# Two attentions of a transformer stack: routing split over two engines, throwaway matmuls in the prologue, and row maxima subtracted by an accumulating matmul

## The reference

```
x = x + linear_attention(layernorm(x))   # 16 heads of 8, the sums run over the sequence positions
x = x + moe(layernorm(x))
x = x + softmax_attention(layernorm(x))  # 16 heads of 8, scores / sqrt(8), softmax over 256 keys
x = x + moe(layernorm(x))
```

## Time and profile before

| | us |
|---|---|
| median of 3 runs | 580.54 (578.9 to 585.16) |
| the profiled execution | 574.57 |
| its span, first to last instruction | 572.8 |
| PE busy | 517.6 (90%) |
| DVE busy | 432.7 (76%) |
| ACT busy | 344.8 (60%) |
| POOL busy | 290.0 (51%) |
| mean granted clock of PE | 0.971 of full |

### The profile page before, as it was taken

How to read it: one execution, slowest core, us unless ns; L and a number is a source line. 1 busy time by engine, 2 the same in 40 slices (tenths; PEclk the granted TensorE clock), 3 DMA queues, 4 the chain that set the end, 5 groups by cost and what they waited for, 6 DMA issues and landing times. The chain is left out here.

```text
span 572.8 us, 11532 instructions
## 1 busy us (share of the span) xinstructions
PE 517.6 (90%) x3757; PEld 390.4 (68%) x3757; DVE 432.7 (76%) x1105; ACT 344.8 (60%) x607; POOL 290.0 (51%) x276
## 2 busy tenths in 40 slices
PE   3878887899999999999788898988999999999996
PEld 3555564577888888888454555645678888888884
DVE  3678798569798898567677887989479796886663
ACT  3676746456555655666457767676865655555553
POOL 4765572146666756777421305020166656666664
PEclk9799988899999999999779999999999999999999
DMA  6358870213454344235641524310442444354340
GB/s 168 114 185 263 245 249 2 72 62 98 107 116 127 92 119 121 98 112 180 200 117 51 185 75 143 116 39 3 62 106 97 109 135 124 103 137 132 95 143 20
DMA packets 48549, 67.60 MB, mean 118 GB/s; under 512 B 6625, under 2 KB 18930, under 8 KB 48498
## 3 DMA queue, kind: packets, MB, share of 16 engines
q1 hardware_dynamic: 45392, 66.47, 39.9%
q10 hardware_dynamic: 3106, 0.48, 0.5%
HBM read 53.56 MB, written 13.37 MB: 117 GB/s over the span
## 5 line engine op out<-in xcount | busy, mean ns | idle before, releaser
L639 POOL TENSOR_TENSOR KS<-PT,QS 128x512 fp32r<-128x512 f32 x144 | 186.2, 1294 | 118.1 <-ACT QS L836 106.1
L831 ACT ACTIVATE bank<-bank 128x512 f32<-128x512 f32 x128 | 74.5, 582 | 98.5 <-PE bank L856 97.9
L1562 DVE TENSOR_TENSOR PT<-CS,bank 128x512 f32<-128x512 f32 x128 | 87.4, 683 | 45.1 <-PE bank L856 44.3
L854 PE MATMUL bank<-XH,WH 128*128 128x512 f32 (+1 forms) x288 | 115.4, 401 | 1.7 <-DVE PT L1434 1.5
L856 PE MATMUL bank<-XH,WL 128*128 128x512 f32 (+1 forms) x288 | 112.9, 392 | 0.0
L855 PE MATMUL bank<-XL,WH 128*128 128x512 f32 (+1 forms) x288 | 112.6, 391 | 0.0
L836 ACT ACTIVATE QS<-PT 128x512 fp32r<-128x512 f32 x144 | 90.1, 626 | 12.2 <-DVE PT L1567 11.8
L1458 DVE TENSOR_REDUCE MEXP<-bank 128x4 f32<-128x1024 f32 x64 | 78.2, 1223 | 22.8 <-PE bank L966 22.1
L1567 DVE TENSOR_TENSOR PT<-PT,bank 128x512 f32<-128x512 f32 x128 | 88.0, 687 | 9.5 <-ACT bank L831 1.6
L750 ACT ACTIVATE PT<-bank 128x1024 f32<-128x1024 f32 x64 | 65.6, 1025 | 40.1 <-PE bank L998 39.8
L1021 PE MATMUL bank<-PT,V 128*32 128x256 f32 (+1 forms) x1024 | 64.6, 372 | 0.3 <-ACT OTS L760 0.3
(11 more groups left out here) (185 smaller groups left out, 770.6 us busy)
## 6 DMA issues: line engine op xcount, KB each, us to landing
CS<-combine_rows SPq DMA_DIRECT2D x128, 256.0 KB, 3.2
head_rows<-HP SPq DMA_DIRECT2D x28, 256.0 KB, 3.0
QS<-head_rows SPq DMA_DIRECT2D x28, 256.0 KB, 2.7
KS<-head_rows SPq DMA_DIRECT2D x28, 256.0 KB, 3.0
head_rows<-PHI SPq DMA_DIRECT2D x14, 256.0 KB, 3.1
out_dram<-X SPq DMA_DIRECT2D x4, 256.0 KB, 3.7
stage<-in_L_ffn_gate_w_dram SPq DMA_DIRECT2D x5, 192.0 KB, 3.8
stage<-in_L_ffn_up_w_dram SPq DMA_DIRECT2D x5, 192.0 KB, 4.0
```

Of the source, the lines that this page charges most:

```text
L639: pool.tensor_tensor(GL[:, (u - 1) % 3, :], GG[:, (u - 1) % 3, :], GH[:, (u - 1) % 3, :].bitcast(f32), ALU.subtract).then_inc(F.gl, 1)
L831: act.activation(TH[:, u, :] if u < SHARED else G[u % 3][:, :], G[u % 3][:, :], ACT.Silu).then_inc(F.th, 1)
L854: pe.matmul(out, wh, vh, start=start, stop=False)
L1562: dve.tensor_tensor(ab, CS[:, e % CBUFS, :], U[u % 3][:, :], ALU.mult).then_inc(F.b, 1)
```

## The change

- Routing: elementwise links move to POOL (`route` in its block), sorts and reductions stay on DVE. There are still 18 links a chunk; parts 0, 2, 3, 5, 7 are POOL's and 1 to 6 DVE's, so the chain goes back and forth. On DVE the two best of each group come from 16 MAX8 instructions (one per tile and group) on SB8, where seven small min and max operations stood. Parts 0 and 7 of DVE are gone.
- Weights are split in 18 units of 384 columns at their own slots; ACT does its share after the block copies of the slot.
- The 1e-5 of the denominators comes in as the bias of ACT's copy (L760); L1481 and its semaphore go.
- XN of the chunks after an attention: ACT does tiles 0 and 1, POOL tiles 2 and 3.
- PE gets 26 + 4 + 2 + 3 throwaway matmuls in the prologue and 8 in slot 2. DVE does the statistics of chunks 1 and 2 and the bias rows before the first features, and makes head key 0 itself. The features of chunk 1 and its layer norm come a slot earlier; ACT's features come after its block copies.
- The first unit of an expert stage comes a slot later.
- Second attention: Q2 is now only the turned maxima, copied by ACT (`maxima_rows`), and each of the 8 matmuls of scores less maxima becomes two that accumulate: 24 rows of KS and QS, and 25 rows of KS and Q2. The two heads of a pair alternate.

Core of the diff (DVE's reduced `route` and constants are left out):

```diff
-        PIECE_SLOTS = [9, 11, 16, 18, 24, 26]
-        ROUTE_SLOTS = [{24: (0,), 25: (1,), 26: (2,), 27: (3,), 28: (4,), 29: (5,), 30: (6,), 31: (7,)},
-                       {27: (0,), 28: (1,), 29: (2,), 30: (3,), 31: (4,), 32: (5,), 33: (6, 7)}]
-        NORM0_STATS = {1: 1, 4: 2, 8: 3}
-        NORM0_POWER = {2: 1, 5: 2, 9: 3}
-        NORM0_SCALE = {3: 1, 6: 2, 10: 3}
-        NORM0_TURN = {4: 1, 8: 2, 12: 3}
-        NORM0_LOW = {5: 1, 9: 2, 13: 3}
+        PIECE_SLOTS = [9, 10, 10, 11, 11, 12, 15, 15, 17, 17, 19, 19, 23, 23, 25, 25, 27, 27]
+        POOL_ROUTE_SLOTS = [{24: (0,), 25: (2,), 27: (3,), 29: (5,), 30: (7,)},
+                            {27: (0,), 28: (2,), 29: (3,), 31: (5,), 32: (7,)}]
+        DVE_ROUTE_SLOTS = [{25: (1,), 26: (2, 3), 28: (4, 5), 30: (6,)},
+                           {28: (1,), 29: (2, 3), 30: (4, 5), 32: (6,)}]
+        NORM0_STATS = {8: 3}
+        NORM0_POWER = {1: 1, 5: 2, 9: 3}
+        NORM0_SCALE = {2: 1, 6: 2, 10: 3}
+        NORM0_TURN = {3: 1, 8: 2, 12: 3}
+        NORM0_LOW = {4: 1, 9: 2, 13: 3}
+        LINKS = 18
...
-        for c, n in ((1, 5), (2, 12), (3, 19)):
+        for c, n in ((1, 4), (2, 12), (3, 19)):
             FEATURE_SLOT[n], FEATURE_SLOT[n + 1] = (0, c), (1, c)
-        UNIT_SLOT = [35, 36]
-        LATE_SLOTS = [{1: (35, 36), 2: (37,), 3: (38, 39), 4: (40,), 5: (41,), 6: (42,), 7: (43,), 8: (44,), 9: (45,),
+        UNIT_SLOT = [36, 37]
+        LATE_SLOTS = [{1: (36,), 2: (37,), 3: (38, 39), 4: (40,), 5: (41,), 6: (42,), 7: (43,), 8: (44,), 9: (45,),
                        10: (46,)},
-                      {1: (36,), 2: (37,), 3: (38, 39), 4: (40,), 5: (41, 42), 6: (43,), 7: (44,),
...
+                      {2: (37,), 3: (38, 39), 4: (40,), 5: (41, 42), 6: (43,), 7: (44,),
...
+        POOL_ROUTE_AT = {False: {4: (0,), 5: (2,), 7: (3,), 9: (5,), 11: (7,)},
+                         True: {0: (0,), 2: (2,), 4: (3,), 6: (5,), 8: (7,)}}
+        DVE_ROUTE_AT = {False: {5: (1,), 6: (2, 3), 8: (4, 5), 10: (6,)},
+                        True: {1: (1,), 3: (2, 3), 5: (4, 5), 7: (6,)}}
...
+            def route(A, c, part):
+                base = c * LINKS
+                def link(k, instr):
+                    instr.then_inc(A.rv, 1)
+                def after(k):
+                    pool.wait_ge(A.rv, base + k)
+                by_group = SB8[:, :, 0:EPG]
+                if part == 0:
+                    pool.wait_ge(A.th, c + 1)
+                    link(1, pool.tensor_tensor(T4[:, :, :], TH64[:, bass.ds(c * CT, CT), :], HALF[:, 0:1].unsqueeze(2)
+                                               .broadcast_to([P, CT, EXPERTS]), ALU.mult))
+                    after(1)
+                    link(2, pool.tensor_tensor(SC[:, :, :], T4[:, :, :], HALF[:, 0:1].unsqueeze(2)
+                                               .broadcast_to([P, CT, EXPERTS]), ALU.add))
+                    after(2)
+                    link(3, pool.tensor_tensor(by_group.rearrange("p (t g) e -> p t g e", g=GROUPS),
+                                               SC[:, :, :].rearrange("p t (g e) -> p t g e", e=EPG),
+                                               RB[:, :].rearrange("p (g e) -> p g e", e=EPG).unsqueeze(1)
+                                               .broadcast_to([P, CT, GROUPS, EPG]), ALU.add))
+                if part == 2:
+                    after(4)
+                    link(5, pool.tensor_tensor(GE[:, :, 0:GROUPS], TOP[:, :, 0].rearrange("p (t g) -> p t g", g=GROUPS),
+                                               TOP[:, :, 1].rearrange("p (t g) -> p t g", g=GROUPS), ALU.add))
+                if part == 3:
+                    after(7)
+                    pool.tensor_tensor(pool_junk[:, :], NEG[:, 0:1], NEG[:, 0:1], ALU.mult)
+                    link(8, pool.tensor_scalar(GMK[:, :, :], GR[:, :, 0:GROUPS], -BIG / 3, None, ALU.is_lt))
+                    after(8)
+                    gmk = GMK[:, :, :].rearrange("p t g -> p (t g)")
+                    pool.tensor_tensor(T1[:, :], gmk, NEG[:, 0:1].broadcast_to([P, CT * GROUPS]), ALU.add)
+                    link(9, pool.tensor_tensor(T4[:, :, :].rearrange("p t (g e) -> p (t g) e", e=EPG), by_group,
+                                               gmk.unsqueeze(2).broadcast_to([P, CT * GROUPS, EPG]), ALU.mult))
+                    after(9)
+                    link(10, pool.tensor_tensor(ME[:, :, 0:EXPERTS].rearrange("p t (g e) -> p t g e", e=EPG),
+                                               T4[:, :, :].rearrange("p t (g e) -> p t g e", e=EPG),
+                                               T1[:, :].rearrange("p (t g) -> p t g", g=GROUPS).unsqueeze(3)
+                                               .broadcast_to([P, CT, GROUPS, EPG]), ALU.add))
...
+                if c:
+                    pool.wait_ge(L.xt, c)
+                for t in range(CT // 2, CT):
+                    i = pool.tensor_scalar(XN[:, t, :], X[:, c * CT + t, :], MV[:, t, 0:1], RS[:, t:t + 1],
+                                           ALU.subtract, ALU.mult)
+                i.then_inc(L.xn, 1)
...
-                    if 2 <= n < 2 + HG:
-                        head_keys(n - 2)
+                    if 2 <= n < 1 + HG:
+                        head_keys(n - 1)
...
+                def maxima_rows(i):
+                    if not 0 <= i < ITEMS:
+                        return
+                    act.wait_ge(A.mt, i + 1)
+                    if i >= 2:
+                        act.wait_ge(A.s2[0], 2 * i - 2)
+                    act.activation(Q2[:, i % 2, :], MT[:, 0:SEQ], ACT.Copy).then_inc(A.q2, 1)
...
+                            act.activation(OTS[:, :], OT[:, :], ACT.Identity, bias=SUM_EPS[:, 0:1]).then_inc(A.ot, 1)
...
-                    for t in range(CT):
+                    for t in range(CT // 2):
...
+            def keep_busy(times):
+                for _ in range(times):
+                    pe.matmul(BANK[1][:, 0:P], ident[:, :], ident[:, :], start=True, stop=True)
             pe.wait_ge(s_id, 2)
+            keep_busy(26)
             pe.wait_ge(s_nat, 16 * 4)
             for m in range(4):
                 i = pe.transpose(BANK[0][:, P * m:P * (m + 1)], nat[:, m, :], ident[:, :])
             i.then_inc(s_wt, 1)
+            keep_busy(4)
...
             first_turn(0)
+            keep_busy(2)
...
             pe.transpose(BANK[3][:, 0:EXPERTS], nat[0:EXPERTS, 8, :], ident[0:EXPERTS, 0:EXPERTS]).then_inc(s_wt, 1)
+            keep_busy(3)
...
-                    pe.wait_ge(A.q2, i + 1)
                     if i + 2 - x < ITEMS:
                         pe.wait_ge(A.mx[x], i + 3 - x)
                     else:
                         pe.wait_ge(A.ex[x], i)
-                    for h in (2 * x, 2 * x + 1):
-                        r = slice(32 * h, 32 * h + 3 * HD + 1)
-                        for t in range(2):
-                            o = SEQ * b + P * t
+                    pe.wait_ge(A.q2, i + 1)
+                    heads = (2 * x, 2 * x + 1)
+                    for t in range(2):
+                        o = SEQ * b + P * t
+                        for h in heads:
+                            r = slice(32 * h, 32 * h + 3 * HD)
+                            pe.matmul(S[h][:, SEQ * t:SEQ * (t + 1)], KS[r, j, o:o + P], QS[r, j, SEQ * b:SEQ * (b + 1)],
+                                      start=True, stop=False)
+                        for h in heads:
+                            r = slice(32 * h, 32 * h + 3 * HD + 1)
                             m = pe.matmul(S[h][:, SEQ * t:SEQ * (t + 1)], KS[r, j, o:o + P], Q2[r, i % 2, :],
-                                          start=True, stop=True)
-                        m.then_inc(A.s2[x], 1)
+                                          start=False, stop=True)
+                            if t:
+                                m.then_inc(A.s2[x], 1)
...
+                        if c == 0:
+                            keep_busy(8)
...
+            bias_rows()
+            first_stats(1)
+            first_stats(2)
...
-                def queries_with_maxima(i):
-                    if not 0 <= i < ITEMS:
-                        return
-                    cc, j, b = item(i)
-                    dve.wait_ge(A.mt, i + 1)
-                    if i >= 2:
-                        dve.wait_ge(A.s2[0], 2 * i - 2)
-                    dve.tensor_tensor(Q2[:, i % 2, :], MT[:, 0:SEQ], QS[:, j, SEQ * b:SEQ * (b + 1)].bitcast(f32),
-                                      ALU.add).then_inc(A.q2, 1)
...
-                        dve.tensor_scalar(DEN[:, :, :], o[:, :, :, HD], DEN_EPS, None, ALU.add).then_inc(A.dn, 1)
-                        dve.wait_ge(A.dn, q + 1)
-                        dve.reciprocal(RDEN[:, :, :], DEN[:, :, :]).then_inc(A.rd, 1)
-                    else:
-                        dve.reciprocal(RDEN[:, :, :], o[:, :, :, HD]).then_inc(A.rd, 1)
+                    dve.reciprocal(RDEN[:, :, :], o[:, :, :, HD]).then_inc(A.rd, 1)
...
```

(36 more changed lines are left out.)

146 lines of the change are left out of this document (61 added, 85 removed).

## The result

The changed kernel takes 593.41 us (median of 5 runs, 587.58 to 596.13) against 580.54 before (the median of 5 runs too, not of 3 as the table ahead says). The ratio is 1.0247, with a 95% interval of 1.0201 to 1.0293. The profiled executions took 587.58 us (span 585.8) and 574.57 us; that of the changed kernel is the fastest of its five.

A forecast was written before the change was run, and what follows sets the result against it. The prediction took PE to fill the expert stages and a PE-ACT chain to set the second attention's slot. First attention -4.8 and second +9.0 made +4.2 us, 574.57 to 578.8 profiled, 584.8 as median; range 572 to 594.

The forecast's parts named there:

- rival 2: Second attention: weight loads show in the packs, another 0.48 us a slot, +9 us on the forecast, 594; chance 0.08.
- Prologue, +2.0: First attention's start: net cost between +1.2 us if the clock stays up and +4 if it falls; +2.0 taken.
- given back about 3 us, if the clock stays up: Prologue: PE's busy 6.23 us at low clock, 17.5 to 24.3, becomes about 3 us shorter if the clock stays up.
- rival 1: Prologue: clock still low after the throwaways, PE free at 13.0 us, 5.2 us on the forecast, 590; chance 0.13.
- DVE's order, 1.0 us late: Prologue: two sets of statistics and bias rows ahead of PQ, 2.8 us in a hole of 1.77, 1.0 late.
- The middle, -5.6: First attention: PE's waits for head rows, block copies, XN and OTOK shrink, sum 6.95 us, 0.8 of it taken.
- XN in halves -0.8: First attention's middle: splitting XN between ACT and POOL takes 0.8 us off PE's wait of 2.43.
- Low clocks, -1.7: First attention: low stretches at 82.3 and 109.7 give half back each, with a chance of one half, -1.7 us.
- Second attention, +9.0: Second attention: packs grow from 0.51 to 0.73 us, undisturbed slots from 3.54 to 3.98; +9.0 us together.
- the upper bound: Second attention: each added matmul step has its weight load in the open, 0.46 us a pack, 0.92 a slot.
- rival 3: Second attention: DVE is the bound, slots fall to about 3.8 us, all -7.8 us, 572.7; chance 0.17.
- rival 4: First attention: all listed waits and both low stretches go, prologue free, -12 against +9, 577.5 us; chance 0.17.

The follow-up runs named there:

- after: The kernel with the whole change, against the kernel before: median 593.41 us, ratio 1.0247.
- g1: The changed kernel without any throwaway matmuls: ratio 1.0122 to the kernel before.
- f1: The changed kernel with the second attention as before and no throwaway matmuls: ratio 0.9951 to the kernel before.
- e1: The changed kernel with the second attention as before, all throwaways in: ratio 1.0114 to the kernel before.
- e3: The changed kernel without the key-query products in the second pack, so it computes something else: ratio 1.0148 to the kernel before.
- e4: The changed kernel with VectorE instead of ScalarE copying the maxima: ratio 1.0301 to the kernel before.
- f4: f1 with bias rows and statistics of chunks 1 and 2 behind the features, and L1406 five slots later: ratio 1.0005 to the kernel before.
- g2: f1 with the low halves of the query and key weights (L1406) five slots later: ratio 0.9898 to the kernel before.
- f3: e1 with the low halves of the query and key weights (L1406) five slots later: ratio 1.0039 to the kernel before.
- g3: g2 with ScalarE's table load a slot later, behind its normalised rows: ratio 0.9887 to the kernel before.
- e2: The kernel before with the change of the second attention alone: ratio 1.019 to the kernel before.
- f2: e1 with bias rows and the statistics and power of chunks 1 and 2 back behind the features: ratio 1.0129 to the kernel before.

## Why the prediction was off

The forecast was +4.2 us. Measured were +13.0 us between the profiled executions, 12.9 between the medians and 14 by the ratio. The range held the median of 593.41, but by luck: its upper end of 594 was that of rival 2, which fell.

Differences of ratios, times 577 us (the time of the kernel before beside these runs), give what each part cost:

| part | forecast | measured | from |
|---|---|---|---|
| throwaways | +1.0 (3.2 late, 2.2 given back) | +7.2 | after less g1 |
| rest of the first attention | -5.8 | -2.8 | f1 |
| second attention | +9.0 | +9.9 | g1 less f1 |

The first and third are good to about 4 us, the second to 2. Two steps failed: what the throwaways cost, by most, and what the middle of the first attention gives.

- *Prologue, +2.0*: the first failed step. "First products 4.2 us late" was right, 4.3. But "given back about 3 us, if the clock stays up", of which the sum took 2.2, didn't come: the low stretch only came later, at 32.9, and in e1, e3 and e4, which share this prologue, the masks of item 0 started at 22.3 to 24.8, up to 8 us later than before. With the throwaways in, the mean clock was lower and not higher. In size it is rival 1 (5.2 us more), but not by its sign (transposes after 11 us; they came at 8.9 to 10.3): the transposes behind the 26 calls ran in 0.60 us, at the higher level, and the clock fell later, so that only its second half came true, the last 8 calls at the low clock, 3.6 us in e1.
- *DVE's order, 1.0 us late*: I had it as a cost and it is a gain, since the turn of chunk 1 depends on it (f4 against g2). Its bias rows took 1.18 us beside POOL's L627, which the sum hadn't in it.
- *The middle, -5.6*: the second failed step. I added up waits that would go, took 0.8 of them, and named none that would come. The 1.50, 1.40 and 1.70 us went; the 2.24 and 1.21 came, of which f3 traces the first to operations moved into an occupied slot, and 1.55 and 2.43 stayed. The 1.55 I had put on POOL's long piece, which had held up L1342. No routing operation of DVE is slow any more, as forecast, but the wait is 1.59: DVE's statistics (84.77 to 86.05) and 16 MAX8 (to 87.17) now stand ahead of the masks, and the sum had the MAX8 at nothing, as a like exchange for what they replaced. No run tests this reading of the trace. "XN in halves -0.8" failed since ACT's copies and table load set its start (g3).
- *Low clocks, -1.7*: ahead of the second attention one stretch of four went, 3.4 us. But from the first maxima on the low clock lasted 27 us instead of 16, and over the whole execution it was 8 us more.
- *Second attention, +9.0*: right in mechanism, and in size within what the runs can tell. The pack took 0.75 us (forecast 0.73), undisturbed slots 3.95 to 4.00 (3.98), the mean 4.19 (4.2). The copy cost nothing (0.1 to 0.3 taken). The sum over the slots has 25 where there are 24, 0.35 us. The profiled execution had 12.0 us instead of 9.0. The step "at the low clock +2.0" was 33.89 - 30.04 = 3.9 us between the maxima of items 0 and 7. Of these some 2 are due to the longer low stretch: e1, without the longer packs and at the low clock for as long, took 32.09. The last part grew by 1.9 us in place of -0.4; in g1, with the same second attention, it took 175.50 us too, in e2 174.74. Why isn't shown.
- *Weight loads in the open*, the upper bound and rival 2: fell. The bound was a pack of 0.51 + 2 x 0.23 = 0.97 us. The Trainium skill (TensorE: Matmul & The Clock Gate, Part 3, The mechanism) says that a weight load overlaps a running matmul only when the row group differs. The trace doesn't agree: the eight matmuls in two row groups took 0.75 us, 0.12 for each further step of a row group.
- *DVE is the bound* (rival 3): fell, by e4 and e2. *The first attention gives all of it* (rival 4, -12): fell, by f1.

What the experiments leave: shown is that the throwaways, all together, cost 0.7% in the kernel before and 1.2 to 1.6% in the changed one, and that the mean granted clock is then lower. Where in the kernel it is lower isn't shown: in the profiled executions the low clock lasted 14 to 31 us up to the first maxima with all throwaways in and 10 to 21 without, and 24 to 48 against 16 to 37 after them, so the ranges overlap. Why it is lower, and whether a part of the throwaways does this alone, stays open.

## What to carry to other kernels

In a ring through two engines, a cheap operation taken off a third engine at the price of work on the ring is a loss. Time the ring's links first: here 0.41 us off VectorE a slot bought nothing, and 0.24 us more in each half slot cost 10 us. When an operation moves a slot, list what already stands in its new slot, on the same engine and on the one that shares its work: the largest new wait was such a meeting, and moving one of the two away again took it from 2.24 to 0.75 us. Throwaway work that is meant to warm an engine up belongs only where the engine would wait for data anyway. Here 26 calls at the very start, while the first weights are still on their way, cost nothing that shows; 8 calls ahead of real work are a delay of 1.95 us, and of 3.62 when the clock is low after all. And with changes of 1 to 2%, split the loss by runs of its parts before a sum is believed: one profiled execution showed the first attention 0.6 us late at item 31, where others with the same first attention had it 5 to 8 us late.

## What the runs showed of the hardware

In the first 14 us the durations of matmuls double (0.60 against 1.09 us for four transposes) while the granted clock reads 1.00 in both kernels, so this column doesn't tell the speed of a cold start. Executions differ in this: with the same prologue the features took 0.40 us a product in the kernel before and 0.63 in e2.

Two VectorE operations took several times their time while a GpSimd tensor_tensor ran, and ended 0.15 and 0.2 us after it: the copy of two one-partition rows (1x128) 1.18 us instead of 0.32 (f2), and the 128x128 subtraction of L1406 1.38 us instead of 0.29 (f3).

Eight accumulating matmuls of 256 columns in two row groups, with eight weight loads, take 0.75 us, 0.24 us more than four.

Runs of one kernel spread by up to 1.5%, and the longer ones mostly have the lower mean granted clock: 567.6 us of span at 0.968 and 573.5 at 0.953 in g2.
